# The second attention of a vision tower: its products on GpSimd, groups 1 and 2 in one set of steps, group 2's weighted values summed on VectorE, and ten idle products at the closing norm

## The reference

```python
def _L1_attn_ref(x, in_proj_weight, in_proj_bias, logit_scale, head_scale, out_w, out_b):
    L, N, C = x.shape                       # 4 images, 189 places, 192
    qkv = x @ in_proj_weight.T + in_proj_bias
    q, k, v = jnp.split(qkv, 3, axis=-1)    # 12 heads of 16
    ...
    attn = jnp.einsum('nhld,nhmd->nhlm', _normalize(q), _normalize(k))
    ls = jnp.exp(jnp.minimum(logit_scale, LOGIT_SCALE_MAX))
    attn = jax.nn.softmax(attn * ls[None], axis=-1)
    o = jnp.einsum('nhlm,nhmd->nhld', attn, v)
    o = o * head_scale[None]
    return o.transpose(2, 0, 1, 3).reshape(L, N, C) @ out_w.T + out_b
```

## Time and the profile before

| | before |
|---|---|
| median of 3 runs | 483.2 us (478.06 to 486.17) |
| the profiled execution | 477.98 us, of which the span is 476.1 us |
| mean granted clock of TensorE | 0.973 of full speed |
| busy: PE, PEld | 445.4 us, 374.2 us |
| busy: DVE, ACT, POOL | 229.3 us, 161.2 us, 94.9 us |
| PE in the chain that ended last | 79% |
| the stretch of the change | about 253 to 302 us |

### The profile page before, as it was taken

How to read it: one execution, slowest core, us unless ns; L and a number is a source line. 1 busy time by engine, 2 the same in 40 slices (tenths; PEclk the granted TensorE clock), 3 DMA queues, 4 the chain that set the end, 5 groups by cost and what they waited for, 6 DMA issues and landing times.

```text
span 476.1 us, 8591 instructions
## 1 busy us (share of the span) xinstructions
PE 445.4 (94%) x3315; PEld 374.2 (79%) x3315; DVE 229.3 (48%) x725; ACT 161.2 (34%) x341; POOL 94.9 (20%) x104
## 2 busy tenths in 40 slices
PE   5989987999999999999999689999999989999996
PEld 3776656765886799999997489876776789899986
DVE  3352448587496832222234996543534357311223
ACT  2245643356765212222115502423313533121120
POOL 0010000013021265553200012200000002773220
PEclk9969999999999999999999889999999979999999
DMA  7983000000023489999755100210000030667463
GB/s 234 293 193 69 1 1 1 1 17 18 0 73 124 105 214 297 265 260 243 160 142 155 50 1 2 92 56 1 3 1 1 1 100 9 171 159 194 121 186 99
DMA packets 42267, 48.99 MB, mean 103 GB/s; under 512 B 7711, under 2 KB 39771, under 8 KB 42228
## 3 DMA queue, kind: packets, MB, share of 16 engines
q1 hardware_dynamic: 38356, 44.41, 35.4%
q0 software_dynamic: 3872, 4.04, 3.3%
HBM read 41.39 MB, written 8.40 MB: 105 GB/s over the span
## 4 chain that ended last, share of the span: by engine, by line
PE 79%; DVE 12%; DMA 4%; issue 3%; ACT 2%; SPq 0%; DVEq 0%; POOL 0%; POOLq 0%
PE bank L528 54%; PE bank L533 3%; PE bank L1008 2%; DMA raw<-in_mfc 2%; PE bank L1031 1%; PE bank L1034 1%; DMA big<-xd,row 1%; PE bank L1047 1%; DVE lg L2080 1%; DVE big L2070 1%; PE bank L1011 1%; PE bank L905 1%; PE bank L549 1%; PE bank L639 1%; PE bank L1014 1%
## 5 line engine op out<-in xcount | busy, mean ns | idle before, releaser
L528 PE MATMUL bank<-mt,raw 96*128 96x128 f32 x432 | 51.3, 275 | 0.3 <-issue 0.3
L528 PEld LDWEIGHTS bank<-mt,raw 96*128 96x128 f32 x432 | 49.7, 192 | 0.5 <-issue 0.5
L528 PE MATMUL bank<-raw,big 128*95 128x192 f32 (+1 forms) x228 | 38.4, 327 | 0.9 <-issue 0.9
L528 PEld LDWEIGHTS bank<-raw,big 128*95 128x95 f32 (+1 forms) x228 | 36.5, 167 | 1.5 <-issue 1.5
L528 PE MATMUL bank<-big,raw 96*128 96x190 f32 x192 | 32.4, 325 | 1.1 <-issue 0.7
L528 PEld LDWEIGHTS bank<-big,raw 96*128 96x128 f32 x192 | 31.0, 189 | 1.6 <-issue 0.8
L2026 DVE TENSOR_TENSOR mt<-bank,mt 128x384 f32<-128x384 f32 x18 | 10.0, 558 | 44.1 <-PE bank L528 44.1
L1519 ACT ACTIVATE big<-bank 128x380 f32<-128x380 f32 (+1 forms) x32 | 13.1, 408 | 51.8 <-PE bank L528 51.8
L533 PE MATMUL bank<-ident 128*128 128x128 f32 x148 | 22.7, 319 | 4.0 <-ACT lg L1445 4.0
L533 PEld LDWEIGHTS bank<-ident 128*128 128x128 f32 x148 | 21.8, 233 | 4.5 <-ACT lg L1445 4.5
L528 PE MATMUL bank<-big 128*36 128x192 f32 (+2 forms) x88 | 17.7, 365 | 5.3 <-DMA tokb<-in_tokb 5.3
(11 more groups left out here) (481 smaller groups left out, 909.3 us busy)
## 6 DMA issues: line engine op xcount, KB each, us to landing
raw<-in_fgu SPq DMA_DIRECT2D x19, 576.0 KB, 7.5
raw<-in_fdn SPq DMA_DIRECT2D x19, 288.0 KB, 6.1
raw<-in_mfc SPq DMA_DIRECT2D x8, 576.0 KB, 6.9
raw<-in_mpj SPq DMA_DIRECT2D x8, 576.0 KB, 5.5
big<-in_w SPq DMA_DIRECT2D x5, 576.0 KB, 8.3
yd<-big SPq DMA_DIRECT2D x2, 1134.0 KB
xd<-xn SPq DMA_DIRECT2D x4, 567.0 KB
big<-in_p SPq DMA_DIRECT2D x3, 432.0 KB, 4.6
```

What stands on the lines that cost most here:

```text
L528: mm = te.matmul(o, l, r, start=first and k == 0, stop=last and k == len(pairs) - 1)
```

## The change

- The twelve cells come in another order: image 0 of all three groups first, then images 1 to 3 of group 0, of group 1, of group 2. The first cell stands ahead of the third pair of transposes, whose three idle products are gone.
- The products of groups 1 and 2 are made by GpSimd, each in five pieces as cells come in; so are the four products of `values(0)`. New semaphores: `prod_r`, `o_pool`, `shares_r`, `pad_set`.
- `logits` and the four short steps of the shares (now `shares`) treat groups 1 and 2 together; group 0 stays by itself. `ssum2` is laid out anew for that (q and k apart), and the two rows that group 1 doesn't fill are set to one by GpSimd at the kernel's start.
- Group 2's weighted values are summed over `m` by VectorE in two additions (`summed`), so TensorE has 8 products there and not 32.
- The idle products after the cells wait for `prod_r` and are 12 instead of 16, those at the closing norm are 10 instead of 20.
- `r2` is made from the variance itself, and one square root and one reciprocal treat `r1` and `r2` together. All of `xn` is made first, then all of `h2`.

```diff
-        ring.add(LN("ln2"))
-        ring.add([(("qk", r, l), "s") for r in range(3) for l in range(4)])
+        QK = [(0, 0), (1, 0), (2, 0)] + [(r, l) for r in range(3) for l in range(1, 4)]
+        ring.add(LN("ln2")[:2] + [(("qk", 0, 0), "s")] + LN("ln2")[2:] + [(("qk", r, l), "s") for r, l in QK[1:]])
         ring.add([(("oT", r, b), "s") for r in range(3) for b in range(2)])
...
-            for g, idle in enumerate((5, 6, 3)):
...
+            for g, idle in enumerate((5, 6)):
                 tr_pairs("ln2", xn, 2 * NT, idle, groups=range(g, g + 1), low=True)
             te.wait_ge(*loaded("qkv"))
...
+            cells_of(0, 0)
+            tr_pairs("ln2", xn, 2 * NT, groups=range(2, 3), low=True)
+            for r, l in QK[1:]:
+                cells_of(r, l)
+            te.wait_ge(prod_r, 2)
...
-                        spin(ps, 16)
+                        spin(ps, 12)
                     for l in (2 * b, 2 * b + 1):
-                        te.wait_ge(o_ready, 4 * r + l + 1)
+                        if r == 0:
+                            te.wait_ge(o_pool, l + 1)
+                        else:
+                            te.wait_ge(o_ready, l + 1)
...
-                te.wait_ge(o_ready, 9 + l)
-                for m in range(4):
-                    for z in range(2):
-                        p = slice(64 * z, 64 * z + 64)
-                        mm = te.matmul(pz[z][0:DH, l * 64:(l + 1) * 64], prod[2][p, l, m, :], ident[p, p], start=m == 0, stop=m == 3)
-                        if l == m == 3:
-                            mm.then_inc(bank_full, 1)
+                if l == 0:
+                    te.wait_ge(o_ready, 5)
+                for z in range(2):
+                    p = slice(64 * z, 64 * z + 64)
+                    mm = te.matmul(pz[z][0:DH, l * 64:(l + 1) * 64], prod[2][p, l, 0, :], ident[p, p], start=True, stop=True)
+                    if l == 3:
+                        mm.then_inc(bank_full, 1)
...
-            tr_pairs("ln3", xn, 3 * NT, 20)
+            tr_pairs("ln3", xn, 3 * NT, 10)
...
+            cells_out(0, 0)
+            evac_pairs("ln2", xT, range(2, 3))
+            for r, l in QK[1:]:
+                cells_out(r, l)
+                if (r, l) == (2, 1):
+                    cell_norms(slice(0, 1))
+            cell_norms(slice(1, 3))
+            for z, rs in enumerate((slice(0, 1), slice(1, 3))):
+                p = TT if z == 0 else 128
+                ac.wait_ge(lexp_in, z + 1)
+                ac.activation(lg2[0:p, rs, :, :, :], lg2[0:p, rs, :, :, :], ACT.Exp).then_inc(lexp, 1)
...
             def dots(r):
                 p = LP[r][0]
-                own()
+                if r == 0:
+                    own()
+                else:
+                    ve.wait_ge(prod_r, r)
...
+            def logits(rs):
+                p, nr = TT if rs.stop == 1 else 128, rs.stop - rs.start
...
+            def shares(rs):
+                p, nr = TT if rs.stop == 1 else 128, rs.stop - rs.start
...
+            def summed(r):
+                v = prod[r][0:LP[r][0], :, :, :]
+                own()
+                st(ve.tensor_tensor(v[:, :, 0:2, :], v[:, :, 0:2, :], v[:, :, 2:4, :], ALU.add))
+                own()
+                ve.tensor_tensor(v[:, :, 0, :], v[:, :, 0, :], v[:, :, 1, :], ALU.add).then_inc(o_ready, 1)
...
             ve.wait_ge(*ring.done(("qk", 1, 3)))
-            products(1, every, every)
             squares(1)
             dots(1)
             ve.wait_ge(*ring.done(("qk", 2, 3)))
             squares(2)
-            logits(0)
-            products(2, every, every)
+            logits(slice(0, 1))
             dots(2)
-            logits(1)
-            values(0)
-            logits(2)
+            shares(slice(0, 1))
+            logits(slice(1, 3))
+            shares(slice(1, 3))
+            ve.wait_ge(shares_r, 2)
             values(1)
             values(2)
+            summed(2)
...
-            ve.tensor_scalar(r1, var, EPS, None, ALU.add).then_inc(var_ready, 1)
+            st(ve.tensor_scalar(r1, var, EPS, None, ALU.add))
+            ve.tensor_scalar(r2, var, 1.0 + EPS, EPS * EPS, ALU.mult, ALU.add).then_inc(var_ready, 1)
             ve.wait_ge(std_ready, 5)
-            st(ve.reciprocal(r1, r1))
-            own()
-            st(ve.tensor_tensor(r2, r1, r1, ALU.mult))
-            own()
-            st(ve.tensor_tensor(r2, r2, var, ALU.mult))
-            own()
-            ve.tensor_scalar(r2, r2, EPS, None, ALU.add).then_inc(var_ready, 1)
+            own()
+            st(ve.reciprocal(rstd[:, 0:2 * NT], rstd[:, 0:2 * NT]))
+            own()
 
             def normed(dst, t, r):
                 return ve.tensor_scalar(dst[:, t, :], h[:, t, :], mv[:, t, 0:1], r[:, t:t + 1], ALU.subtract, ALU.mult)
-            for t in range(2):
-                st(normed(h2, t, r1))
-            ve.wait_ge(std_ready, 6)
-            st(ve.reciprocal(r2, r2))
-            own()
-            st(ve.tensor_tensor(r2, r2, r1, ALU.mult))
-            own()
             for t in range(NT):
                 normed(xn, t, r2).then_inc(xn_ready, 1)
-            for t in range(2, NT):
+            for t in range(NT):
...
+            for r in range(1, 3):
+                po.wait_ge(*ring.done(("qk", r, 1)))
+                products(r, slice(0, 2), slice(0, 2))
+                po.wait_ge(*ring.done(("qk", r, 2)))
+                products(r, slice(2, 3), slice(0, 3))
+                products(r, slice(0, 2), slice(2, 3))
+                po.wait_ge(*ring.done(("qk", r, 3)))
+                products(r, slice(3, 4), slice(0, 4))
+                products(r, slice(0, 3), slice(3, 4)).then_inc(prod_r, 1)
+            def values(r):
+                p = LP[r][0]
+                for l in range(4):
+                    po.tensor_tensor(prod[r][0:p, l, :, :].rearrange("p m (h d) -> p m h d", h=AHH),
+                                     lg2[0:p, r, l, :, :].unsqueeze(3).to_broadcast([p, 4, AHH, AD]),
+                                     qkv[r][0:p, :, 2 * DH:3 * DH].rearrange("p m (h d) -> p m h d", h=AHH), ALU.mult).then_inc(o_pool, 1)
+            po.wait_ge(shares_r, 1)
+            values(0)
...
```

More of the change, by code:

```diff
@@ L1199, in quad, with evac_pairs @@
                 return banks[:, c0:c0 + 4 * BANK].rearrange("p (g n) -> p g n", g=4)
-            def evac_pairs(name, dst):
-                for g in range(NT // 2):
+            def evac_pairs(name, dst, groups=range(NT // 2)):
+                for g in groups:
                     ps = full((name, g))
@@ L1463, in evac_scaled @@
                     it.then_inc(emptied_s, 1)
-            for n in (5, 6):
-                ac.wait_ge(var_ready, n)
-                r = rstd[:, (n - 5) * NT:(n - 4) * NT]
-                ac.activation(r, r, ACT.Sqrt).then_inc(std_ready, 1)
+            ac.wait_ge(var_ready, 5)
+            ac.activation(rstd[:, 0:2 * NT], rstd[:, 0:2 * NT], ACT.Sqrt).then_inc(std_ready, 1)
             ac.wait_ge(*loaded("l1"))
@@ L2074, in squares @@
                 p = LP[r][0]
[L2075 removed]
+                if r == 0:
+                    ve.wait_ge(pad_set, 2)
+                ve.tensor_reduce(ssum2[0:p, :, r, :, :].rearrange("p a l h -> p l a h"),
+                                 sqk[r][0:p, :, :].rearrange("p l (a h d) -> p l a h d", a=2, d=AD), X, ALU.add).then_inc(ssum_r, 1)
             def dots(r):
                 p = LP[r][0]
[L2079 removed]
+                if r == 0:
+                    own()
+                else:
+                    ve.wait_ge(prod_r, r)
                 st(ve.tensor_reduce(lg2[0:p, r, :, :, :].rearrange("p l m h -> p (l m h)"),
                                     prod[r][0:p, :, :, :].rearrange("p l m (h d) -> p (l m h) d", d=AD), X, ALU.add))
[L2083 to L2086 removed]
+            def logits(rs):
+                p, nr = TT if rs.stop == 1 else 128, rs.stop - rs.start
+                ssum, lg = ssum2[0:p, :, rs, :, :], lg2[0:p, rs, :, :, :]
+                qs, ks = ssum2[0:p, 0, rs, :, :], ssum2[0:p, 1, rs, :, :]
+                by_row, by_cell = lg.rearrange("p r l m h -> p r l (m h)"), lg.rearrange("p r l m h -> p (r l) m h")
+                spread = lambda x: x.rearrange("p r l h -> p (r l) h").unsqueeze(2).to_broadcast([p, 4 * nr, 4, AHH])
+                ve.wait_ge(snorm, 1 + rs.start)
                 st(ve.tensor_scalar(ssum, ssum, 1e-12, None, ALU.max))
@@ L2399, in _, with products, values @@
                                       bounds_check=2 * T - 1, oob_is_err=False).then_inc(sca1, 16)
+            def products(r, ls, ms):
+                p, nl, nm = LP[r][0], ls.stop - ls.start, ms.stop - ms.start
+                shape = [p, nl, nm, DH]
+                return po.tensor_tensor(prod[r][0:p, ls, ms, :], qkv[r][0:p, ls, 0:DH].unsqueeze(2).to_broadcast(shape),
+                                        qkv[r][0:p, ms, DH:2 * DH].unsqueeze(1).to_broadcast(shape), ALU.mult)
+            for r in range(1, 3):
[7 more added lines that the diff above has]
```

(9 more changed lines are left out.)

101 lines of the change are left out of this document (47 added, 54 removed).

## The result

The changed kernel takes 473.99 us (median of 4 runs, 472.85 to 475.85) against 480.63 us for the kernel before in the same session (4 runs, 477.95 to 486.17): a ratio of 0.9875, with a 95% interval of 0.9829 to 0.9920. That is faster by 1.25%, and inside 2%. The profiled execution took 472.85 us with a span of 471.0 us and a mean clock of 0.976; before, these were 477.98, 476.1 and 0.973.

A forecast was written before the change was run, and what follows sets the result against it. VectorE's work was taken to price the attention up to the projection, the closing norm being a second stage. Gains of 1.1 + 1.5 = 2.6 us took the median from 483.2 to 480.6 us; range 474 to 486.

The forecast's parts named there:

- The cells: Ahead of the attention's products: third pair's idle products and copy wait go, 1.39 us; twelfth cell out at 267.1.
- GpSimd's products: Groups 1 and 2's products on GpSimd: 4.15 us a group, starting behind VectorE's last product, second group ready at 271.2.
- rival 2: GpSimd slower on repeated operands: at 1.5 times, 3.5 us slower, 486.7 us; chance 0.18.
- The hold on the steps of group 0: Logits 0 on VectorE: two of seven steps before 271.2, the end at 272.5 instead of 271.4.
- The hold on the joint steps: Joint logits of groups 1 and 2 beside GpSimd's group 0 values: VectorE waits together 2.7 us, end 280.85.
- TensorE behind it: After VectorE's end at 288.25: products 0.73, copies 0.64, passing on 0.1; projection at 289.75, 1.1 us gained.
- Rival 3: Clock falls a second time, to 0.50 at the projection: 4.2 us on the forecast, 484.8 us; chance 0.10.
- Rival 1: GpSimd and VectorE run side by side, nobody held: 6.8 us gained, 476.4 us; chance 0.24 with mixtures.
- The norm: Closing norm: xn starts 1.35 us earlier, ten idle products out of the way, 1.5 us gained.
- The step to the median: Whole run: median of the runs taken as 5.2 us above the profiled execution, so 483.2 us before.

The follow-up runs named there:

- cells_late: Changed kernel with the third pair of transposes, its idle products and copy wait ahead of all cells again; xn to projection 37.47 us, ratio 0.9971.
- values0_vector: Changed kernel with group 0's weighted values back on VectorE; xn to projection 36.30 us, ratio 0.9867.
- clock_kept: Changed kernel with nine idle products added ahead of group 1's sums; xn to projection 35.72 us, median 478.68 us, no ratio worked out.
- idle20: Changed kernel with twenty idle products in the closing norm instead of ten; projection to q, k, v 10.23 us, ratio 0.9960.
- tensor_sums2: Changed kernel with group 2's weighted values summed by TensorE again in 32 small products; xn to projection 38.00 us, ratio 0.9873.
- attention_alone: Changed kernel with the closing norm as before; xn to projection 36.14 us, projection to q, k, v 10.19 us, ratio 0.9900.
- turns: Changed kernel with group 0's shares ahead of group 2's dots on VectorE; xn to projection 35.13 us, ratio 0.9895.
- turns_fewer: Changed kernel with group 0's shares ahead of group 2's dots, nine idle products before group 1's sums, first block 9 not 12; stage 34.89 us, ratio 0.9894.
- products_vector: Changed kernel with groups 1 and 2's products back on VectorE, idle products awaiting the first exponential; xn to projection 38.00 us, ratio 0.9952.

## Why the prediction was right, and which sizes were off

The forecast was 480.6 us, 2.6 less than before, with nearly all the chance within 2%. The sign came out so, and the change is within 2%, as in every case that the forecast had named. The median of 473.99 is 0.01 us below the low edge of the range, 474, so the range held only to the rounding; it is 6.6 us below the forecast, and 6.6 below the median of before in the same session. By stages 3.8 us of that are the change: 1.48 at the norm, forecast 1.5, and 2.31 at the attention, forecast 1.1. The parts, on before's scale (1.15 us added to the new starts):

- **The cells: right.** The twelfth cell is out at 267.21, forecast 267.1, and group 0's second product starts at 261.20, forecast 261.2. cells_late gives 1.32 us of the stage for the forecast's 1.39.
- **GpSimd's products: right in length.** Pieces of 384 numbers take 0.99 us and of 288 0.79, as forecast, repeated operands or not: rival 2 is out. But the first started beside VectorE's last product and not behind it, so both groups are ready at 270.46 instead of 271.2. GpSimd was held in it only 0.27 us (1.26 against 0.99).
- **The hold on the steps of group 0: too high.** I had two of the seven steps done before 271.2 and the rest behind it, 1.1 us late. Only the first was held for long (0.69 us for 0.18), since most of the seven came after GpSimd's end: 2.46 us instead of 1.91, so 0.55.
- **The hold on the joint steps: the largest wrong term of the sum.** The prediction said "waits of 0.2, 1.0, 1.0 and 0.5, together 2.7 us"; values0_vector gives 1.81. Each piece of the values takes 0.84 us, not 0.99, and GpSimd is over after 3.35 us, so that three steps are held (by 0.62, 0.67 and 0.52) and line 2119 runs free. The logits end at 278.92 instead of 280.85, and from there to the last addition every term fits: exponential 0.43 (0.44), shares 1.65 (1.58), values 3.84 (3.85), additions 1.55 (1.55). VectorE is 1.8 us ahead of the forecast at the end, 1.1 of them already when the joint steps start (274.28 instead of 275.4).
- **TensorE behind it: wrong in the other direction.** "It keeps up with groups 0 and 1" did not hold. Rival 3's mechanism, a second fall of the clock, did occur, but at group 1's sums and not at the projection, so that it cost 0.43 us (clock_kept) and not 4.2: at 0.50 the sums ran most of their time beside VectorE's values. The projection starts 2.16 us after the last addition, forecast 1.5. Without the fall of the clock it is 1.74 (clock_kept), since the eight products take 0.90 us and not 0.73. With VectorE 1.83 us ahead of the forecast, 1.83 - 0.66 = 1.17, the difference between 2.3 and 1.1.
- **Rival 1 (nobody is held, 6.8 us): wrong.** Its time of 476.4 us was nearer to the median, for another reason. values0_vector shows the hold, and the stages 3.8 us.
- **The norm: right**, and by its own reasoning: idle20 shows that the idle products were the bound, and the transposes now wait for `xn`, which starts 0.79 us after the first step on the variance, forecast 0.8.
- **The step to the median.** I took 5.2 us between median and profiled execution from three runs. Before's later medians (480.4 to 481.0) stand 2.4 to 3.0 us above that profile. Of the 6.6 us between 480.6 and 473.99, some 2.6 come from this, 1.2 from the stages, and the rest is not explained by either.

Not settled: 6.6 and 5.6 us of median against 3.8 us of stages. The intervals of the changed kernel reach to 0.9920 and 0.9939, and 3.8 us is 0.9921, so it is at their edge; values0_vector and tensor_sums2 have 3.6 and 1.9 us of stages, which would be 0.9924 and 0.9960, and intervals that end below, at 0.9914 and 0.9950. In the other direction, attention_alone and idle20 have the same two stage lengths within 0.05 us and ratios of 0.9900 and 0.9960, with intervals that overlap. Of the kernel before there is one profile, of an execution 2.4 to 3.0 us below its medians, so whether its other parts are usually longer can't be read. The last part of the span, 174.2 to 180.0 us, points to dips of the clock elsewhere, but no run here isolates one.

What the runs say of each part, from the changed kernel: cells 1.32 us, products on GpSimd 1.85, additions 1.85, values of group 0 on GpSimd 0.15. They share cover and don't add up to 2.31. What the joint steps alone give was not run, nor 12 idle products for 16 behind the cells. Left unused: 1.02 us by turns, and 1.26 with nine idle products on top; the medians don't resolve either (475.0 to 475.6 us against 473.99 and 475.40), and the rest of their span was longer, so none is shown to beat the changed kernel.

## What to carry to other kernels

Work that is moved from VectorE to an idle GpSimd can be paid back by VectorE's own two-input steps beside it: of group 0's values 1.81 of 1.96 us were, while the products of groups 1 and 2 spared VectorE 2.27 of 3.5 us. Lay GpSimd's pieces beside sums, reciprocals or waits, as turns did, and let the last piece end there. Idle products ahead of a short chain can be the bound themselves, so when the chain is shortened, take some of them away as well. Measure an edit of 1 us by a stage between two fixed instructions, because the whole run of this kernel moves by several microseconds from one execution to the next.

## What the runs showed of the hardware

- **Who holds whom, by kind of step.** Beside GpSimd's products, a two-input VectorE step of 48 to 192 numbers lasts about as long as one of GpSimd's pieces (0.83 to 1.02 us for 0.21 to 0.36). GpSimd's pieces stay at 0.84, the last at 0.95 (0.84 in turns_fewer): the cost is nearly one-sided here, where I had counted on turns. "SBUF — State Buffer" of the Trainium skill (Who interferes with whom) has the pair held for whole instructions by whoever comes first; VectorE's rows agree. GpSimd lost 0.11 us in all, less than VectorE's steps take alone (0.21 to 0.36 us each), and no run here says why.
- **A step with one input can be held too.** The TENSOR_SCALAR of 48 numbers took 0.69 us beside GpSimd's product, and 0.18 alone. I had counted only two-input steps. The same section says so of this operation in a two-port mode; that the step ran in one is not shown here. Sums and the reciprocal of 96 numbers (0.75 us beside GpSimd and without it) were not held.
- **Clearing memory doesn't hold.** The two steps at 279.21 and 279.45 us ran beside GpSimd's MEMSET (278.23 to 279.64) and took 0.21 and 0.36 us, as without it.
- **GpSimd on repeated operands.** 384 numbers took 0.99 us in the products and 0.84 in the weighted values. Both have a repeated operand; I know of no row that says why they differ.
- **A short wait may or may not cost the clock.** After 2.38 us without work (2.46 in turns, 2.68 in tensor_sums2, 2.69 in cells_late) the clock fell to 0.50 in the sums behind it (5.00 to 5.32 us); after 2.69 in products_vector it did not (3.65 us). What decides it is open.
